# Filling the spread tile of a selective scan from SBUF instead of through DRAM, with ScalarE issuing the transfers

## The chip, the cores and the metric

The kernel runs on one core of one Trainium2 chip. The metric is the time of one execution on the device in microseconds (us); the kernel before was run three times, and the median counts. A profile of one further execution belongs to it, and all rows below come from that.

## The reference, cut to what matters

The program computes `x + s * silu(g)` for 2 sequences of 1024 tokens and 512 features in float32. `s` is a Mamba-like selective scan on the normalised input, with 1024 inner channels and 16 states per channel; `g` is a mixture of 8 experts of which each token uses 2. The part that the change touches is the scan:

```python
dt = softplus(ts @ W_dt.T + b_dt)          # one step size per token and channel
def step(state, inp):
    dt_t, B_t, C_t, u_t = inp
    dA = exp(dt_t[..., None] * A)          # 16 decays per channel
    state = state * dA + (dt_t * u_t)[..., None] * B_t[:, None, :]
    return state, einsum('bdn,bn->bd', state, C_t)
```

Every channel's `dt` and `dt * u` are needed 16 times, once for each of its 16 states.

## The kernel before, in words

**Tiling.** The 2048 tokens are cut into 4 chunks of 512 (two chunks to a sequence), and the 1024 inner channels into 8 groups of 128. One group in one chunk is called a tile; there are 32, numbered n = 8c + t for chunk c and group t. A tile needs 128 channels x 16 states x 512 tokens of recurrence. The 128 SBUF partitions hold 32 channels x 4 states at a time, so a tile takes 16 scans of 128x512: 4 quads (q = 0 to 3, the states) with 4 blocks each (r = 0 to 3, the channels, 32 at a time). A quad has a running number m = 4n + q.

**The spread tile.** The scans want each channel's row four times over, on four neighbouring partitions. `dtu` holds, on one partition per channel, two rows of 512 numbers: `dt` and `u`, which is dt times x. `rep` holds the same data spread: four blocks r, in each of them 32 channels x 4 copies on the 128 partitions. `rep` has two halves, used by even and odd tiles. It comes about in these steps for tile k:

- VectorE makes `dt` in PSUM and `u` in SBUF (`times_x`, L1163 to L1172).
- ScalarE copies `dt` from PSUM into `dtu` (`keep_dt`, L781 to L785), and stores `dtu` to the DRAM tensor `rep_rows` with one DMA of 512 KB (`keep_rows`, L861 to L866).
- SyncE (SP) waits for that store (`s_dtu`), and for tiles from 2 on also for the last reader of the half (`decay_ok`, `drive_ok`), and issues four DMAs of 512 KB from `rep_rows`, each reading 32 rows of 4 KB four times (`spread`, L415 to L423). They report to `s_rep`, two of them to each of its two semaphores.

`dtu` exists once. So both writers of the next tile's `dtu`, `times_x` on VectorE and `keep_dt` on ScalarE, wait until the store of the tile before has landed.

**The scan of a quad m.** POOL (GpSimd) multiplies the u half of `rep` by B into `drive`, 128x2048 at once (`drives`, L594 to L606, a ring of 4 slots, each free again when TensorE has summed it). ScalarE makes the decays, `exp(A * dt)`, from the dt half of `rep` into four PSUM banks `sc`, two banks at a time (`decays(m, h)`, L799 to L819): it waits for VectorE's product that last read the banks, copies the last state out, and runs two exponentials. VectorE scans (`scan(m, r)`, L1194 to L1209), and VectorE or POOL multiplies by C (L1217; `low_products` L618). TensorE sums the states into `y_ps` (`sums`, L1496 to L1502), and VectorE multiplies by the gate (`gate_tile`, L1225 to L1229).

**Everything beside it.** In the gaps of each tile TensorE also projects the next chunk's x (L1396), the gate (L1460), the expert slots (L1474, L1485) and the output (L1532). ScalarE does the convolution's first tap and x copies (`copy_x`, L715 to L729), the softplus of the tile after next (`softplus`, L777), SiLU between two loads of its function table (L956 to L970), copies of expert slots (L828, L837) with their stores (L844), and more. VectorE does three convolution taps (L1136) for each group of the next chunk.

**What sets the order.** All engines' orders are written out by hand, one stream each. SP's stream is a single one as well: a wait in it holds back all loads behind it. In a tile n the ScalarE stream is: `decays(m, 1)`, `keep_dt(n+1)`, copy of an expert slot, `diagonal(n)`, `keep_rows(n+1)`, a store of an expert slot, `decays(m+1, 0)`, `copy_x` in some tiles, `decays(m+1, 1)`, `copy_slot_T`, `decays(m+2, 0)`, table load, SiLUs, table load, `decays(m+2, 1)`, and so on (L925 to L996). In the last group of a chunk `keep_dt` and `keep_rows` come behind `decays(m+1, 0)`. SP's stream in a tile has `spread(n+1)`, then the load of the gate's weights, then expert slots and their weights (L483 to L546). At the start, before tile 0, VectorE runs `rms(0)`, `step_sizes(0)`, `route_ranks()`, `step_sizes(1)`, `route_rows()` and then the first scans (L1255 to L1265); SP issues `spread(0)` behind the stores of the normalised rows `xn_rows` (`s_xn`) and the transposes (`tr_mm`), which read the memory of `rep` under its other name `x_in` (L471 to L481).

Of the kernel before, what the change touches and what calls it, by code (L numbers as in the profile page):

```python
# [5 lines left out]
F32 = mybir.dt.float32  # L6
# [5 lines left out]
P = 128  # L12
# [3 lines left out]
TC = 512  # L16
# [100 lines left out]
def scan_moe(nc, x, wx_in, wg_in, wdt_in, wxp, wring, gate_w, means, a_log, conv_w, conv_b, d_skip,  # L117
             route_consts, bc_dram, rep_rows, xn_rows, xnT_rows, slot_x, slot_rows, s_rows, out):
    with ExitStack() as ctx:
# [6 lines left out]
        def sem(name):  # L126
            return ctx.enter_context(nc.semaphore(name))
# [127 lines left out]
        s_wdt = sem("s_wdt")  # L255
        s_dtu = sem("s_dtu")
        s_wr = [sem(f"s_wr{s}") for s in range(2)]
# [66 lines left out]
        def drives_done(eng, count):  # L324
            eng.wait_ge(drive_ok, count)
# [8 lines left out]
        def rep_landed(eng, k):  # L334
            for h in range(2):
                eng.wait_ge(s_rep[k % 2][h], REP // 2 * (k // 2 + 1))

        @block.sync
        def _(sp):
# [74 lines left out]

            def spread(k):  # L415
                sp.wait_ge(s_dtu, 16 * (k + 1))
                if k >= 2:
                    sp.wait_ge(decay_ok, UNITS * (k - 1))
                    drives_done(sp, NQ * (k - 1))
                for r in range(NR):  # L420
                    rows = rep_rows[k % 2, CH * r:CH * (r + 1), :].rearrange("c (o f) -> c o f", o=1)
                    sp.dma_start(rep[:, k % 2, r, :, :].rearrange("p k t -> p (k t)"),
                                 rows.broadcast_to([CH, NG, 2 * TC])).then_inc(s_rep[k % 2][r // 2], 16)  # L423

            def store_rows(c):
# [48 lines left out]
            sp.wait_ge(tr_mm, 16)  # L474
            spread(0)
            spread_c(0, 0)
# [6 lines left out]
            for n in range(TILES):  # L483
# [23 lines left out]
                if n + 1 < TILES:  # L507
                    spread(n + 1)
                    load_w_g(n + 1)
# [188 lines left out]
        def _(act):  # L698
# [82 lines left out]
            def keep_dt(k):  # L781
                act.wait_ge(dt_ok, k + 1)
                if k:
                    act.wait_ge(s_dtu, 16 * k)
                act.copy(dt, dt_ps[:, :]).then_inc(dt_cp, 1)  # L785
# [74 lines left out]

            def keep_rows(k):  # L861
                act.wait_ge(dt_cp, k + 1)
                act.wait_ge(dt_ok, k + 1)
                if k >= 2:
                    rep_landed(act, k - 2)
                act.dma_start(rep_rows[k % 2], dtu[:, :, :].rearrange("p k t -> p (k t)")).then_inc(s_dtu, 16)  # L866

# [48 lines left out]
            keep_dt(0)  # L916
            keep_rows(0)
            softplus(1)
# [6 lines left out]
            for n in range(TILES):  # L925
# [16 lines left out]
                if t < NT - 1:  # L942
                    keep_rows(n + 1)
                store_slot(b, left_slot)
# [4 lines left out]
                if chunk_end:  # L949
                    keep_dt(n + 1)  # L950
                    keep_rows(n + 1)
                if early is not None:
# [49 lines left out]
        def _(dve):  # L1002
# [160 lines left out]
            def times_x(k):  # L1163
                c, t = divmod(k, NT)
                if pe_log(k):
                    dve.wait_ge(log_mm, pe_logs(k + 1))
                else:
                    dve.wait_ge(sp_ok, k + 1 - pe_logs(k))
                dve.wait_ge(x_ok, k + 1)
                if k:  # L1170
                    dve.wait_ge(s_dtu, 16 * k)
                dve.tensor_tensor(u, dt_ps[:, :], xy[:, c % 2, t, :], ALU.mult).then_inc(dt_ok, 1)  # L1172
# [11 lines left out]
            def plus_log(k):  # L1184
                dve.wait_ge(part_ok, 2 * (k - pe_logs(k)) + 2)
                dve.tensor_tensor(dt_ps[:, :], t_l[:, :], dt_ps[:, :], ALU.subtract).then_inc(sp_ok, 1)

            def step_sizes(k):
                larger_part(k)
                less_rounding(k)  # L1190
                plus_log(k)
                times_x(k)

            def scan(m, r):  # L1194
                n, q = divmod(m, NQ)
                c, t = divmod(n, NT)
                if m == 0 and r == 0:
                    dve.wait_ge(first_half, 1)
                elif m == 0 or r == 0:
                    drives_done(dve, m + 1)  # L1200
                follows = c % PER_ROW > 0
                if follows:
                    dve.wait_ge(state_ok, kept_states(m - NQ * NT) + r // 2 + 1)
                lo = column(t, q, r)
                to = drive[:, m % RING, r, :] if r < 2 and on_pool(m) else sc[:, r, :]
                dve.wait_ge(decay_ok, NR * m + r + 1)
                dve.tensor_tensor_scan(to, sc[:, r, :], drive[:, m % RING, r, :],  # L1207
                                       state[:, lo:lo + 1] if follows else 0.0,
                                       ALU.mult, ALU.add).then_inc(scan_ok, 1)  # L1209
# [47 lines left out]
            route_ranks()  # L1257
            step_sizes(1)
            route_rows()
            scan(0, 0)  # L1260
            scan(0, 1)
# [434 lines left out]
```

## Time and profile before

| | |
|---|---|
| Median of three runs | 1053.31 us (1052.16, 1053.31, 1054.01) |
| The profiled execution, its own time | 1050.33 us |
| Its span, first to last instruction | 1048.4 us |
| Mean granted TensorE clock | 0.914 |
| Busy: VectorE (DVE) | 983.2 us of the span |
| Busy: POOL | 904.9 us |
| Busy: TensorE (PE) | 853.0 us |
| Busy: ScalarE (ACT) | 728.4 us |

How to read it. Busy time counts instructions that compute; waits, register work and the issue of DMAs are not in it. A queue's own work, as a DMA issue, stands in the trace under the engine's name with a q (ACTq, SPq), with the time for which it holds the engine. "Idle before, releaser" says how long the engine had nothing to run and whose end let it go on. A DMA has a time to landing, counted from its issue to its semaphore. The chain of waits goes back from the last instruction through what released each step.

### The profile page before, as it was taken

What the parts mean: (1) busy time and instruction counts of PE and PEld (TensorE: products, weight loads), DVE (VectorE), ACT (ScalarE), POOL (GpSimd) and SP (SyncE); (2) the same over time, 40 slices, a digit from 0 to 9 for tenths busy, and PEclk for the clock granted to TensorE, in tenths of its full rate; (3) what the DMA queues carried; (4) which work ended last, traced back from release to release, by engine and by line L of the source; (5) the groups of instructions that cost most, each with busy time, mean ns of one, the idle gap of its engine ahead of it and who ended that gap; (6) DMA issues with size and microseconds to landing.
All of it is one profiled execution on the core that took longest, in us unless ns stands there. A gap on an engine that the chain in (4) does not pass through costs nothing.

```text
span 1048.4 us, 10364 instructions
## 1 busy us (share of the span) xinstructions
PE 853.0 (81%) x2756; PEld 317.2 (30%) x2756; DVE 983.2 (94%) x1027; ACT 728.4 (69%) x1281; POOL 904.9 (86%) x320
## 2 busy tenths in 40 slices
PE   8945458989878998999746859989888979988478
PEld 5321113333323343333211313333323323323123
DVE  6779999999999999999999899999999997999996
ACT  3656757888877767888664566888778775767543
POOL 0616899989989998998898988899988989999996
PEclk9986669999989999999976869999999998999778
DMA  9948559887779666675843753866548575664735
GB/s 335 350 154 311 203 200 354 294 298 272 264 271 336 226 226 243 240 276 203 282 116 144 212 209 121 309 236 233 203 178 308 204 255 191 237 237 171 283 54 144
DMA packets 86585, 245.93 MB, mean 235 GB/s; under 512 B 9344, under 2 KB 10752, under 8 KB 79872
## 3 DMA queue, kind: packets, MB, share of 16 engines
q1 hardware_dynamic: 67712, 197.03, 53.0%
q10 hardware_dynamic: 12672, 31.46, 7.6%
q0 software_dynamic: 6144, 16.78, 6.0%
q8 instruction: 23, 0.38, 0.1%
q14 instruction: 34, 0.28, 0.1%
HBM read 183.11 MB, written 62.13 MB: 234 GB/s over the span
## 4 chain that ended last, share of the span: by engine, by line
POOL 22%; DVE 21%; PE 20%; issue 12%; ACT 12%; DMA 10%; SPq 2%; ACTq 0%; DVEq 0%; POOLq 0%
POOL drive L605 13%; DVE sc_ps L1207 7%; DMA rep<-rep_rows 5%; POOL drive L618 4%; ACT sc_ps L818 4%; DVE drive L1207 4%; DVE drive L1217 4%; PE x_ps L1532 3%; PE dt_ps L1460 3%; DMA rep_rows<-dtu 3%; PE f_ps L1485 3%; PE y_ps L1500 2%; PE x_ps L1396 2%; POOL slot_x L569 2%; POOL moe L590 1%
## 5 line engine op out<-in xcount | busy, mean ns | idle before, releaser
L605 POOL TENSOR_TENSOR drive<-rep,b_all 128x2048 f32<-128x2048 f32 x127 | 579.6, 4603 | 37.6 <-DMA rep<-rep_rows 34.0
L818 ACT ACTIVATE sc_ps<-rep,a_neg 128x512 f32<-128x512 f32 x512 | 332.2, 681 | 101.8 <-DVE drive L1217 72.1
L1500 PE MATMUL y_ps<-drive,stack 128*32 128x512 f32 x1024 | 151.6, 668 | 104.1 <-DVE drive L1217 66.2
L618 POOL TENSOR_TENSOR drive<-drive,c_all 128x1024 f32<-128x1024 f32 x92 | 219.8, 2389 | 11.8 <-ACT state L797 9.7
L1207 DVE TENSOR_TENSOR_SCAN sc_ps<-sc_ps,state,drive 128x512 f32<-128x512 f32 x164 | 202.5, 1272 | 5.6 <-ACT sc_ps L818 3.9
L1207 DVE TENSOR_TENSOR_SCAN sc_ps<-sc_ps,drive 128x512 f32<-128x512 f32 x164 | 193.5, 1214 | 10.2 <-ACT sc_ps L818 6.1
L1217 DVE TENSOR_TENSOR drive<-sc_ps,c_all 128x1024 f32<-128x1024 f32 x164 | 199.2, 1215 | 2.8
L1485 PE MATMUL f_ps<-w_ring,xT_slot 128*128 128x512 f32 x368 | 173.0, 614 | 23.4 <-ACT xT_slot L828 22.9
L1460 PE MATMUL dt_ps<-xnT,w_g 128*128 128x512 f32 x232 | 125.1, 689 | 24.1 <-ACT dtu L785 24.1
L1207 DVE TENSOR_TENSOR_SCAN drive<-sc_ps,state,drive 128x512 f32<-128x512 f32 x92 | 113.7, 1267 | 6.6 <-ACT sc_ps L818 6.6
L1207 DVE TENSOR_TENSOR_SCAN drive<-sc_ps,drive 128x512 f32<-128x512 f32 x92 | 109.7, 1208 | 2.0 <-POOL drive L605 0.9
L1485 PEld LDWEIGHTS f_ps<-w_ring,xT_slot 128*128 128x128 f32 x368 | 68.5, 194 | 125.0 <-issue 123.3
L1396 PE MATMUL x_ps<-xnT,w_x 128*128 128x512 f32 x192 | 88.2, 602 | 2.2 <-DMA w_x<-wx_in 1.9
L1532 PE MATMUL x_ps<-w_out,xy 128*128 128x512 f32 x176 | 83.2, 617 | 0.0
L1500 PEld LDWEIGHTS y_ps<-drive,stack 128*32 128x32 f32 x1024 | 21.5, 112 | 197.5 <-issue 140.9
L1460 PEld LDWEIGHTS dt_ps<-xnT,w_g 128*128 128x128 f32 x232 | 48.5, 220 | 105.2 <-issue 105.2
L797 ACT ACTIVATE state<-sc_ps 128x2 f32<-128x2 f32 x82 | 13.8, 169 | 65.9 <-DVE drive L1217 65.6
L1396 PEld LDWEIGHTS x_ps<-xnT,w_x 128*128 128x128 f32 x192 | 35.0, 190 | 54.7 <-issue 51.9
L1532 PEld LDWEIGHTS x_ps<-w_out,xy 128*128 128x128 f32 x176 | 33.1, 195 | 49.9 <-issue 49.3
L828 ACT COPY xT_slot<-f_ps 128x512 f32<-128x512 f32 x46 | 26.5, 576 | 28.3 <-PE f_ps L1474 28.3
L1437 PE MATMUL dt_ps<-dt_in,w_dt 128*128 128x512 f32 x64 | 39.9, 708 | 5.4 <-DVE dt_in L1252 4.2
L640 POOL TENSOR_SCALAR rep<-rep,moe 128x512 f32<-128x512 f32 x8 | 16.5, 2065 | 30.5 <-DVEq L1154 30.5
(189 smaller groups left out, 1048.8 us busy)
## 6 DMA issues: line engine op xcount, KB each, us to landing
rep<-rep_rows SPq DMA_DIRECT2D x128, 512.0 KB, 6.2
w_ring<-wring SPq DMA_DIRECT2D x46, 1024.0 KB, 6.3
rep_rows<-dtu ACTq DMA_DIRECT2D x32, 512.0 KB, 3.1
x_slot<-slot_x SPq DMA_DIRECT2D x46, 256.0 KB, 6.7
slot_rows<-y_slot ACTq DMA_DIRECT2D x46, 256.0 KB, 4.4
w_g<-wg_in SPq DMA_DIRECT2D x32, 256.0 KB, 7.1
w_x<-wx_in SPq DMA_DIRECT2D x24, 256.0 KB, 4.3
slot_x<-zeros SPq DMA_DIRECT2D x1, 5888.0 KB, 20.6
```

What stands on the lines that cost most here:

```text
L605: pool.tensor_tensor(drive[:, m % RING, :, :], rep[:, n % 2, :, 1, :], b_all[:, q:q + 1, :].broadcast_to([P, NR, TC]), ALU.mult).then_inc( ...
L618: pool.tensor_tensor(drive[:, m % RING, 0:2, :], drive[:, m % RING, 0:2, :], c_all[:, q:q + 1, :].broadcast_to([P, 2, TC]), ALU.mult).then ...
L818: act.activation(sc[:, r, :], rep[:, n % 2, r, 0, :], ACT.Exp, scale=a_neg[:, lo:lo + 1]).then_inc(decay_ok, 1)
L828: act.copy(xT_slot[:, :, :], f_ps[:, :].rearrange("p (k t) -> p k t", k=HK)).then_inc(xt_ev, 1)
L1207: dve.tensor_tensor_scan(to, sc[:, r, :], drive[:, m % RING, r, :], state[:, lo:lo + 1] if follows else 0.0, ALU.mult, ALU.add).then_inc(s ...
L1217: dve.tensor_tensor(drive[:, m % RING, 2 * h:2 * h + 2, :], sc[:, 2 * h:2 * h + 2, :], c_all[:, q:q + 1, :].broadcast_to([P, 2, TC]), ALU. ...
L1396: last = pe.matmul(x_bank(j), w(h), xnT[:, c % 2, h, :], start=(h == 0), stop=(h == HK - 1))
L1437: pe.matmul(dt_ps[:, :], w_dt[:, t, :], dt_in[:, :], start=True, stop=True).then_inc(dt_mm, 1)
L1460: mm = pe.matmul(gate_bank(c, t)[:, :], w_g[:, h, :], xnT[:, c % 2, h, :], start=(h == 0), stop=(h == HK - 1))
L1485: last = pe.matmul(f_ps[:, :], xT_slot[:, h, :], w_ring[:, j % 2, h, :], start=(h == 0), stop=(h == HK - 1))
L1500: last = pe.matmul(y_ps[CH * r:CH * (r + 1), :], stack[:, :], drive[:, m % RING, r, :], start=False, stop=(m % NQ == NQ - 1))
L1532: last = pe.matmul(bank, xy[:, c % 2, t, P * i:P * (i + 1)], w_out[:, t, :], start=(t == 0), stop=(t == NT - 1))
```

## The change

The store of `dtu` to DRAM and the tensor `rep_rows` go, and so does the semaphore `s_dtu`. The four DMAs that fill `rep` read `dtu` in SBUF, 32 partitions each, four times over. They are issued from ScalarE's stream, where the store was issued. ScalarE takes over the waits for the last reader of the half. Both writers of `dtu` now wait until the `rep` of the tile before has landed (`rep_landed`), which is when `dtu` is read out. At the start ScalarE takes over the waits for `s_xn` and `tr_mm`, and `times_x(1)`, which now has to wait for `rep` of tile 0, is moved behind `route_rows()`.

```diff
-        s_dtu = sem("s_dtu")
...
-            def spread(k):
-                sp.wait_ge(s_dtu, 16 * (k + 1))
-                if k >= 2:
-                    sp.wait_ge(decay_ok, UNITS * (k - 1))
-                    drives_done(sp, NQ * (k - 1))
-                for r in range(NR):
-                    rows = rep_rows[k % 2, CH * r:CH * (r + 1), :].rearrange("c (o f) -> c o f", o=1)
-                    sp.dma_start(rep[:, k % 2, r, :, :].rearrange("p k t -> p (k t)"),
-                                 rows.broadcast_to([CH, NG, 2 * TC])).then_inc(s_rep[k % 2][r // 2], 16)
...
             sp.wait_ge(s_xn, 16 * 16)
             sp.wait_ge(tr_mm, 16)
-            spread(0)
             spread_c(0, 0)
...
                 if n + 1 < TILES:
-                    spread(n + 1)
                     load_w_g(n + 1)
...
             def keep_dt(k):
                 act.wait_ge(dt_ok, k + 1)
                 if k:
-                    act.wait_ge(s_dtu, 16 * k)
+                    rep_landed(act, k - 1)
                 act.copy(dt, dt_ps[:, :]).then_inc(dt_cp, 1)
...
-            def keep_rows(k):
+            def spread(k):
+                act.wait_ge(dt_ok, k + 1)
                 act.wait_ge(dt_cp, k + 1)
-                act.wait_ge(dt_ok, k + 1)
                 if k >= 2:
-                    rep_landed(act, k - 2)
-                act.dma_start(rep_rows[k % 2], dtu[:, :, :].rearrange("p k t -> p (k t)")).then_inc(s_dtu, 16)
+                    act.wait_ge(decay_ok, UNITS * (k - 1))
+                    drives_done(act, NQ * (k - 1))
+                for r in range(NR):
+                    rows = dtu[CH * r:CH * (r + 1), :, :].rearrange("c k (o t) -> c o (k t)", o=1)
+                    act.dma_start(rep[:, k % 2, r, :, :].rearrange("p k t -> p (k t)"),
+                                 rows.broadcast_to([CH, NG, 2 * TC])).then_inc(s_rep[k % 2][r // 2], 16)
...
             keep_dt(0)
-            keep_rows(0)
+            act.wait_ge(s_xn, 16 * 16)
+            act.wait_ge(tr_mm, 16)
+            spread(0)
...
                 if t < NT - 1:
-                    keep_rows(n + 1)
+                    spread(n + 1)
...
                 if chunk_end:
                     keep_dt(n + 1)
-                    keep_rows(n + 1)
+                    spread(n + 1)
...
             def times_x(k):
...
                 if k:
-                    dve.wait_ge(s_dtu, 16 * k)
+                    rep_landed(dve, k - 1)
...
             route_ranks()
-            step_sizes(1)
+            larger_part(1)
+            less_rounding(1)
+            plus_log(1)
             route_rows()
+            times_x(1)
```

## Rows read from the trace of the kernel before

**Rows 1.** The page, busy time of each engine.
```profile
PE 853.0 (81%) x2756; PEld 317.2 (30%) x2756; DVE 983.2 (94%) x1027; ACT 728.4 (69%) x1281; POOL 904.9 (86%) x320
```

**Rows 2.** VectorE's waits: line, releaser, us in total, times, longest.
```profile
DVE sc_ps L1207 <- ACT sc_ps L818: 10.1, 11, 2.0
...
DVE drive L1207 <- ACT sc_ps L818: 7.3, 8, 4.0
...
DVE sc_ps L1207 <- POOL drive L605: 4.6, 4, 2.1
```

**Rows 3.** POOL's waits, the same columns.
```profile
POOL drive L605 <- DMA rep<-rep_rows: 34.0, 13, 8.3
```

**Rows 4.** The four fills (L422) and the store (L866): issue ns min/median/max, landing.
```profile
L422 SPq DMA_DIRECT2D rep<-rep_rows x128: 513/598/932, 68.2 to 982.7; - x128
...
L866 ACTq DMA_DIRECT2D rep_rows<-dtu x32: 326/326/348, 65.4 to 976.9; - x32
...
DMA to landing us min/median/max: 2.6/3.1/8.8
```

**Rows 5.** Timeline, DMA issues on SP; L367 copies SBUF rows four times over.
```profile
267.22 2.46 SPq L422 DMA_DIRECT2D rep<-rep_rows  x4
...
270.37 0.43 SPq L367 DMA_DIRECT2D slot_x<-zeros  x1
...
295.49 1.82 SPq L431 DMA_DIRECT2D b_all<-bc_rows  x3
```

**Rows 6.** Timeline, VectorE where it waited: start, us, instruction, idle before.
```profile
249.08 2.35 DVE L1207 TENSOR_TENSOR_SCAN sc_ps<-sc_ps,drive 128x512 f32<-128x512 f32 x2 [0.75 <-ACT sc_ps L818]
...
599.38 3.46 DVE L1207 TENSOR_TENSOR_SCAN sc_ps<-sc_ps,drive 128x512 f32<-128x512 f32 x3 [2.12 <-POOL drive L605]
...
878.88 2.46 DVE L1207 TENSOR_TENSOR_SCAN drive<-sc_ps,state,drive 128x512 f32<-128x512 f32 x2 [4.04 <-ACT sc_ps L818]
```

**Rows 7.** Timeline: POOL's first drive of a tile, two of 13 stalls; one store ahead.
```profile
540.79 0.33 ACTq L866 DMA_DIRECT2D rep_rows<-dtu  x1
...
554.67 4.53 POOL L605 TENSOR_TENSOR drive<-rep,b_all 128x2048 f32<-128x2048 f32 x1 [3.23 <-DMA rep<-rep_rows]
...
852.45 4.55 POOL L605 TENSOR_TENSOR drive<-rep,b_all 128x2048 f32<-128x2048 f32 x1 [2.94 <-DMA rep<-rep_rows]
```

**Rows 8.** The chain of waits, 834 to 879 us.
```profile
834.63 7.06 DMA rep_rows<-dtu
...
843.81 8.49 DMA rep<-rep_rows
...
866.16 1.94 PE y_ps L1500 x8
```

**Rows 9.** Busy us (x count) by engine, from store to second table load; 15 stretches.
```profile
205.70:219.00 13.30, 11.68 (x35) 4.86 (x36) 13.30 (x15) 11.60 (x22) 12.09 (x4) 1.00 0.85 296
...
664.70:677.10 12.40, 11.86 (x41) 4.52 (x39) 12.37 (x14) 11.55 (x22) 9.92 (x4) 1.00 0.93 336
...
949.40:960.90 11.50, 11.50 (x42) 4.21 (x40) 9.91 (x10) 8.35 (x13) 11.50 (x5) 1.00 0.78 271
sum 175.40, PE 159.26 PEld 62.06 DVE 172.85 ACT 149.13 POOL 162.44; mean PE 10.62 PEld 4.14 DVE 11.52 ACT 9.94 POOL 10.83
```

The columns are length, then PE, PEld, DVE, ACT, POOL, TensorE's granted clock, DMA share and GB/s.

**Rows 10.** Timeline, tile 6: two waits of ScalarE, its decays, VectorE's scans of them.
```profile
269.01 0.17 ACT L797 ACTIVATE state<-sc_ps 128x2 f32<-128x2 f32 x1 [0.46 <-DVE drive L1217]
...
271.91 0.21 ACT L797 ACTIVATE state<-drive 128x2 f32<-128x2 f32 x1 [0.88 <-DVE drive L1207]
...
277.91 1.30 ACT L818 ACTIVATE sc_ps<-rep,a_neg 128x512 f32<-128x512 f32 x2
...
278.71 2.32 DVE L1207 TENSOR_TENSOR_SCAN sc_ps<-sc_ps,drive 128x512 f32<-128x512 f32 x2
```

**Rows 11.** Page, DMA issues: KB each, median us to landing.
```profile
slot_x<-zeros SPq DMA_DIRECT2D x1, 5888.0 KB, 20.6
```

More of the change, by code:

```diff
@@ L117, in scan_moe @@
 def scan_moe(nc, x, wx_in, wg_in, wdt_in, wxp, wring, gate_w, means, a_log, conv_w, conv_b, d_skip,
-             route_consts, bc_dram, rep_rows, xn_rows, xnT_rows, slot_x, slot_rows, s_rows, out):
+             route_consts, bc_dram, xn_rows, xnT_rows, slot_x, slot_rows, s_rows, out):
     with ExitStack() as ctx:
@@ L1685 @@
     bc = nc.dram_tensor("bc_rows", (NCH, 2 * N, TC), F32, kind="Internal").ap()
-    rep_rows = nc.dram_tensor("rep_rows", (2, P, 2 * TC), F32, kind="Internal").ap()
     xn_rows = nc.dram_tensor("xn_rows", (TOK, H), F32, kind="Internal").ap()
@@ L1692 @@
     out = nc.dram_tensor("out", (TOK, H), F32, kind="ExternalOutput").ap()
-    scan_moe(nc, *aps, bc, rep_rows, xn_rows, xnT_rows, slot_x, slot_rows, s_rows, out)
+    scan_moe(nc, *aps, bc, xn_rows, xnT_rows, slot_x, slot_rows, s_rows, out)
     r = run_bass_kernel_spmd(nc, [arrays], core_ids=[0])
```

## The prediction

> **What bounds the kernel now.** I read the page first: VectorE is busy 983.2 us, 94% of the span, POOL 86%, ScalarE 69% [rows 1]. So a change helps only where it takes away a wait of VectorE, and costs only where it gives VectorE a new one. VectorE's waits came next. Behind the start, most of what it waits for is ScalarE's decays, 10.1 + 7.3 us in 19 waits; POOL's drives cost it 4.6 us in 4 [rows 2]. POOL in turn stands for 34.0 us in 13 waits for the fill of `rep` [rows 3]. This is seven times what VectorE waits for POOL: with four slots in the ring most of POOL's stalls never reach VectorE. Last I read the timeline around `keep_rows`, because that is where ScalarE gets more to do.
>
> **What goes: the way through DRAM.** The store lands in 2.6 to 8.8 us [rows 4], and the fill follows it. In tile 25 the store went out at 834.63 and took 7.06 us; the last of the four fills was issued at 843.81 and landed 8.49 us later, 17.7 us in all, and POOL went on at 852.45 after a wait of 2.94 [rows 7, 8]. POOL had thus been ready 14.9 us behind the store's issue. In tile 15 the same reckoning gives 554.67 - 3.23 - 540.79 = 10.7 us, the tightest sort [rows 7]. Afterwards the path is the issue of four DMAs on ScalarE and one landing. If a fill from SBUF goes as fast as one from DRAM, that is 1.9 us to the fourth issue and about 8.5 to its landing, 10.4 us: no stall in tile 25, next to none in tile 15.
>
> How fast a fill from SBUF is, the trace does not show; no DMA in it reads a few partitions several times into SBUF. Its bounds: at the fast end the rate of the one long read of all partitions, 5888 KB in 20.6 us, 286 GB/s, so 7.3 us for four fills [rows 11]; at the slow end a quarter of that rate, since each fill reads a quarter of the partitions, 29 us. I take 10 to 12 us, near the fills that were measured, because the receiving side and the bytes are theirs.
>
> That the slow end deserves thought is what the Trainium skill says ("SBUF — State Buffer", section on the DMA port swizzle): 32 partitions reach only 8 of 16 ports, and it gives 189 GB/s for partitions 0 to 31; by its figure the four fills would take an estimated 11 us before any contention. No row here shows it.
>
> **What VectorE gets from that.** All of its 4.6 us behind POOL can go [rows 2]. The 0.75 us at 249.08 lie behind a stall of tile 5 [rows 6]. The 4.04 us at 878.88 lie on the chain that runs from the late fill through POOL, `y_ps` and the gate to ScalarE; of them the 2.94 of the stall can go [rows 6 to 8]. At the start the first fill is issued some 3 us earlier, since the store's 2.6 us go; that removes about 1 us. The sum is 4.6 + 0.75 + 2.94 + 1 = 9.3 us. I take 7, because in the tightest tiles a fill of 10 to 12 us leaves part of the stall: in tile 15 a fill 1 us late takes back 1 of the 2.12 us at 599.38 [rows 6]. The bounds are 3 and 10.
>
> **What comes: four long issues for a short one on ScalarE.** A plain issue holds its engine 0.33 us; the four fills hold SP 2.46 us, the first 0.51, those behind it 0.60 each; a single row of L431, which also spreads 32 rows to 128 partitions, says the same, 1.82 for three [rows 4, 5]. An issue that copies one row of SBUF four times on its own partition takes 0.43 behind another [rows 5]. The new form spreads 32 to 128, so I take 2.46. ScalarE gets 2.46 - 0.33 = 2.13 us more a tile, 68 us over 32 fills, of which its waits have to swallow what VectorE is not to see.
>
> Tile 6 shows how. Behind the issue ScalarE waits 0.46 and 0.88 us for VectorE, which swallow 1.34. Then come the first table load, the SiLUs and the second table load, and then the decays at 277.91. Their first exponential ends at about 278.6 and VectorE's scan starts at 278.71 [rows 10]: no slack. So 2.13 - 1.34 - 0.1 = 0.7 us reach VectorE. I followed each tile like this, from its `keep_rows` on, taking off every wait of ScalarE and the slack before each scan, and taking what VectorE was given as given, so that it isn't counted twice. 17 tiles swallow everything. 15 do not: tiles 4 to 8, 12, 13, 15, 19 to 24 and 29. Over their stretches ScalarE is busy 149.1 of 175.4 us; of the 26.3 left, the DMA issues, one or two in each and 0.33 long, take some 8, so that about 18 us of waits stand against 15 x 2.13 = 32 us, and 14 remain; the slacks take another 3 [rows 9]. Result: 11 us. The worst is tile 19, 11.55 busy of 12.40, nothing left but issues: 1.9 us arrive [rows 9]. The cost is steep in the issue's price: with 1.5 us more a tile the same reading gives 4 us, with 1.0 it gives 1, with 2.5 it gives 17. Bounds 1 and 17.
>
> **The rest, at nothing.** SP loses four issues and a wait a tile and so sends weights earlier; nobody waits noticeably for these loads, and the price without cover is a later fill by shared bandwidth, which is in its range. `spread`'s waits on ScalarE are for decays it made itself and drives that VectorE has already begun to scan; behind them stand the slot's store and `decays(m+1, 0)`, which would wait too. `keep_dt` and `times_x` wait for a fill that the running tile has already read. At the start, `times_x(1)` goes behind `route_rows`, the same work in another order, and softplus(1) starts 1.2 us later under the routing work. SP no longer waits for the first store and sends its 4 MB of staging up to 3 us earlier, beside the first fill; that can cost the 1 us counted as gain.
>
> **The sum.** -7 + 11 = +4 us on the profiled execution, 1050.33 to 1054.3. That execution lies 3 us below the median of 1053.31, so the forecast is 1057.3.
>
> **Rivals.** *ScalarE has the room, and the kernel gets faster.* If an issue from SBUF costs 0.43, as that of L367 [rows 5], the four take 1.7 and add 1.3 a tile. The cost is then 2 to 3 us against 8 of gain: 1053.3 - 5.5 = 1048. It decides at about 1.8 us more a tile, where cost and gain are both 7. For it speaks that L367 is the only broadcast from SBUF; against it, that its rows stay on their partition.
> *The fill is slow.* If 32 partitions feed it at half rate, four fills take 7.3 x 2 = 14.6 us [rows 11] and the landing is 16 us behind the first issue. POOL is ready after 10.7 in the tight tiles: stalls of 5 us in about ten, where they are 1 to 4 now. Gain 2, and 4 to 8 us more reach VectorE: +4 + 5 + 6 = +15, 1068. At the quarter rate every tile would stall 10 us or more, over 1200; I leave that outside. The rule of the Trainium skill named above points this way, though by its figure the fill would still land at about 13 us.
> *Nothing measurable.* Gain and cost come out equal, near 8 us each, both within their bounds: 1053.
>
> **How the numbers follow.** Forecast, ScalarE's issues outweigh the shorter path: 0.43, own range 1055.4 to 1062. Faster: 0.28. No change: 0.16, that is within 0.2% or 2.1 us, about what a measurement of this kernel can tell from none. Slow fill: 0.13. Slower by over 0.2% is 0.43 + 0.13 = 0.56. The range reaches from 1046, the faster rival with the full 10 us of gain against 3, to 1067, just short of the slow fill.
>
> **What the profile after would show.** Right: no `rep_rows`; L866's place holds four issues of 2.4 to 2.5 us together; ScalarE's waits for VectorE's L1217 shrink by tens of us; VectorE's waits for L818 rise from 17 to some 25 us, the new ones behind the second table load; POOL's 34.0 us fall below 10. Wrong: issues under 0.45 each (the faster rival), POOL waiting 40 us or more for `rep` with landings above 12 us (the slow fill), or a VectorE that waits more for POOL than for ScalarE.

## The result, and the profile after

The changed kernel takes 1309.65 us (median of 4, 1304.28 to 1315.69) against 1052.91 us (median of 4): the ratio is 1.2439, 95% interval 1.2381 to 1.2497. That is 257 us slower. The forecast was 1057.3 in a range of 1046 to 1067. The sign was right and the size wrong by far.

The page of the kernel after, busy time of each engine, answers to [rows 1]:

```profile
span 1306.1 us, 10334 instructions
...
PE 899.7 (69%) x2756; PEld 337.2 (26%) x2756; DVE 988.9 (76%) x1027; ACT 725.8 (56%) x1281; POOL 905.2 (69%) x320
```

VectorE and ScalarE do the same work, VectorE in 988.9 us against 983.2, so all but some 6 of the 257 us are waits. TensorE does the same work too, in 899.7 us against 853.0, at a mean granted clock of 0.831 against 0.914; the run below that only holds ScalarE (e6) has 0.837. These are the waits of the kernel after (engine, line, releaser: us in total, times, longest); L805 is the decays' line, L856 the fills', L831 the slot stores':

```profile
PE f_ps L1481 <- ACT xT_slot L815: 215.6, 25, 14.5
DVE drive L1200 <- ACT sc_ps L805: 171.2, 31, 11.0
...
ACT sc_ps L805 <- issue: 154.9, 16, 12.2
ACT state L784 <- issue: 150.8, 16, 13.7
...
POOL drive L605 <- ACT state L784: 93.5, 14, 12.4
...
DVE sc_ps L1200 <- ACT sc_ps L805: 65.2, 23, 7.4
...
POOL drive L592 <- DMA rep<-dtu: 22.9, 5, 7.0
```

VectorE waits 236 us for ScalarE's decays, against 17.4 [rows 2]. ScalarE stands still for "issue", 306 us in 32 waits, about one to a tile: it waits for no semaphore, it is issuing a DMA. TensorE and POOL wait for ScalarE as well. POOL's waits for `rep`, on which half of the forecast turned, have even fallen, from 34.0 [rows 3] to 22.9 us: at this pace the fills are rarely late.

The issues themselves, on the line of the fills and then on the line of the slot stores (ns min/median/max; below it the us to landing), answer to [rows 4]:

```profile
L856 ACTq DMA_DIRECT2D rep<-dtu x128: 550/868/4395, 65.6 to 1226.4; - x128
...
DMA to landing us min/median/max: 6.2/10.2/18.7
```

```profile
L831 ACTq DMA_DIRECT2D slot_rows<-y_slot x46: 326/362/5767, 177.5 to 1230.2; - x46
```

The median hides it; one tile shows it. ScalarE's timeline of the kernel after, tile 6 (start, us, instruction, idle before):

```profile
309.54 0.57 ACTq L856 DMA_DIRECT2D rep<-dtu  x1
...
310.14 7.89 ACTq L856 DMA_DIRECT2D rep<-dtu  x3
318.08 5.77 ACTq L831 DMA_DIRECT2D slot_rows<-y_slot  x1
323.89 0.21 ACT L784 ACTIVATE state<-drive 128x2 f32<-128x2 f32 x1 [13.64 <-issue]
```

And VectorE's of the same stretch:

```profile
312.71 1.21 DVE L1210 TENSOR_TENSOR drive<-sc_ps,c_all 128x1024 f32<-128x1024 f32 x1
324.92 1.23 DVE L1200 TENSOR_TENSOR_SCAN drive<-sc_ps,drive 128x512 f32<-128x512 f32 x1 [11.00 <-ACT sc_ps L805]
```

The first two issues of this tile take 0.57 and 0.62 us, as forecast. The third takes 3.9 and the fourth 3.3, and a store of an expert slot that has nothing to do with `rep` takes 5.8 us, because it is next on the same queue (with the fills on SyncE, in e1 below, it takes 0.33 again). As long as an issue lasts, the engine that issues does nothing else: the three slow ones are most of the 13.64 us. Summed over the trace the fills' issues take 246.6 us and the slot stores' 86.9; the store of `dtu` and the slot stores took 10.4 and 15.3 before. That is 9.6 us more a tile.

A second loss stands at the start. `times_x(1)` now waits until the fill of tile 0 has landed:

```profile
85.30 0.69 DVE L1165 TENSOR_TENSOR dtu<-dt_ps,xy 128x512 f32<-128x512 f32 x1 [6.88 <-DMA rep<-dtu]
```

The first scan of tile 0 begins at 85.9 us and not at 77.9, 8.0 us of the 257.

### The profile page after: what moved, and what is told of

It is laid out like the page before. It is cut to its first block and busy times, and to the rows that moved or that the text cites. A ratio compares the mean times of both kernels' runs of the same rounds, so it can differ in the third digit from the quotient of the medians.

```text
span 1306.1 us, 10334 instructions
## 1 busy us (share of the span) xinstructions
PE 899.7 (69%) x2756; PEld 337.2 (26%) x2756; DVE 988.9 (76%) x1027; ACT 725.8 (56%) x1281; POOL 905.2 (69%) x320
## 5 line engine op out<-in xcount | busy, mean ns | idle before, releaser
L805 ACT ACTIVATE sc_ps<-rep,a_neg 128x512 f32<-128x512 f32 x512 | 331.2, 681 | 234.5 <-issue 154.9
L1481 PE MATMUL f_ps<-w_ring,xT_slot 128*128 128x512 f32 x368 | 219.7, 753 | 215.6 <-ACT xT_slot L815 215.6
L1481 PEld LDWEIGHTS f_ps<-w_ring,xT_slot 128*128 128x128 f32 x368 | 86.9, 247 | 344.4 <-issue 344.3
L1456 PE MATMUL dt_ps<-xnT,w_g 128*128 128x512 f32 x232 | 121.3, 672 | 32.4 <-ACT dtu L772 32.4
L1496 PEld LDWEIGHTS y_ps<-drive,stack 128*32 128x32 f32 x1024 | 21.6, 112 | 205.2 <-issue 170.6
L784 ACT ACTIVATE state<-drive 128x2 f32<-128x2 f32 x46 | 9.2, 200 | 105.1 <-issue 100.0
L1129 DVE SCALAR_TENSOR_TENSOR x_ps<-x_pad,cw,x_ps 128x512 f32<-128x512 f32 x54 | 40.2, 744 | 17.0 <-ACT x_ps L714 16.5
## 6 DMA issues: line engine op xcount, KB each, us to landing
rep<-dtu ACTq DMA_DIRECT2D x128, 512.0 KB, 10.2
slot_x<-zeros SPq DMA_DIRECT2D x1, 5888.0 KB, 20.6
```

Of the source, the lines that this page charges most:

```text
L805: act.activation(sc[:, r, :], rep[:, n % 2, r, 0, :], ACT.Exp, scale=a_neg[:, lo:lo + 1]).then_inc(decay_ok, 1)
L1129: dve.scalar_tensor_tensor(out=x_bank(j) if k < K - 1 else xy[:, c % 2, t, :], in0=padded(j)[:, k:k + TC], scalar=cw[:, t * K + k:t * K + ...
L1456: mm = pe.matmul(gate_bank(c, t)[:, :], w_g[:, h, :], xnT[:, c % 2, h, :], start=(h == 0), stop=(h == HK - 1))
L1481: last = pe.matmul(f_ps[:, :], xT_slot[:, h, :], w_ring[:, j % 2, h, :], start=(h == 0), stop=(h == HK - 1))
L1496: last = pe.matmul(y_ps[CH * r:CH * (r + 1), :], stack[:, :], drive[:, m % RING, r, :], start=False, stop=(m % NQ == NQ - 1))
```

## The experiments

Each experiment has a short name, e1 to e10 for kernels and m1, m2 for transfers alone. All times are medians in us; "before" is the kernel before, run beside each on the same chip. Its single runs there lie between 1047.6 and 1056.0, which says how much a difference of a few us between single runs is worth.

### Who holds ScalarE: the source or the queue

e2: only the source of the fills changed, ScalarE issues them:

```diff
+            act.dma_start(first_rep, dtu[:, :, :].rearrange("p k t -> p (k t)")).then_inc(s_dtu, 16)
+            act.wait_ge(s_dtu, 16)
             spread(0)
...
-                    rows = dtu[CH * r:CH * (r + 1), :, :].rearrange("c k (o t) -> c o (k t)", o=1)
+                    rows = first_rep[CH * r:CH * (r + 1), :].rearrange("c (o f) -> c o f", o=1)
```

> The changed kernel with the source of the fills alone exchanged: ScalarE issues the same four DMAs in the same places, but they read 128 rows of 4 KB of a DRAM tensor that is written once, with dt and u of tile 0; so every tile gets the dt and u of tile 0. Theory A (the source is slow): four issues take 2.4 to 2.6 us together, landings 6 to 7 us, and the time is 1050 to 1070 us. Rival B (ScalarE's queue holds fewer transfers than SyncE's, or fills on it are slow in themselves): four issues still take 7 to 9 us and the time stays above 1250 us.

Measured: 1085.0 (one run) against 1049.9. The issues and landings of its fills:

```profile
L857 ACTq DMA_DIRECT2D rep<-first_rep x128: 520/625/1420, 73.7 to 1011.1; - x128
...
DMA to landing us min/median/max: 3.4/6.4/13.9
```

The four issues take 2.4 us in nearly every tile, the very price of the forecast. So ScalarE issues these fills as fast as SyncE did, and the source makes the hold. The time is higher than expected. About 12 us of the 35 are this experiment's own late start: ScalarE waits for the one store, and the first scan begins at 90.3 us instead of 77.9. The other 23 us I put down to the 2.1 us more on ScalarE a tile, less what the shorter path gives back; e10 below, which holds ScalarE 2.4 us, loses 21.6.

e1: the other way round, SyncE issues (`spread` moves to its stream, with its waits) and the source is SBUF:

```diff
             def spread(k):
-                act.wait_ge(dt_ok, k + 1)
+                sp.wait_ge(dt_ok, k + 1)
...
                 if n + 1 < TILES:
+                    spread(n + 1)
                     load_w_g(n + 1)
```

> The changed kernel with its four fills issued by SyncE instead of ScalarE; they still read dtu in SBUF. Theory A (a fill from 32 partitions of SBUF drains slowly, about 4 us each, and the third and fourth issue hold whichever engine issues them until an earlier fill has drained): SyncE's issues of a tile take 7 to 9 us together, as ScalarE's did (7.9 in tile 5 of the changed kernel), the landings stay near 10 us, but ScalarE is free, its slot stores take 0.33 us again, and the kernel comes back to 1060 to 1110 us, with POOL waiting 50 to 150 us for rep. Rival B (it is ScalarE's queue that is slow, not the source): SyncE's issues take 2.5 us together, landings 6 to 7 us, and the time is at or below that of the kernel before, 1040 to 1053 us.

Measured: 1107.12 against 1049.91, ratio 1.0538 (1.0494 to 1.0582). Issues, landings and POOL's waits:

```profile
L422 SPq DMA_DIRECT2D rep<-dtu x128: 547/902/4665, 65.7 to 1039.9; - x128
...
DMA to landing us min/median/max: 6.7/9.9/20.1
```

```profile
POOL drive L605 <- DMA rep<-dtu: 90.1, 17, 12.3
```

The hold follows the source to SyncE: the four issues in tile 1 take 0.55, 0.60, 4.07 and 2.01 us, and in 26 of 32 tiles the third takes 3.9 us or more. There it holds back loads and not decays, and 200 of the 257 us are gone. The other 57 I put down to a second fault: the fills land late, and POOL, no longer slowed by ScalarE, now waits 90 us for them. VectorE's waits bear most of that out: it waits 32.4 us for POOL's drives instead of 5.5, and 14.0 instead of 5.5 for TensorE's sums behind them; another 11.5 us are for a part of the softplus that TensorE adds, in four tiles. The loads held back on SyncE cost little: TensorE's waits for DMAs (matmuls and weight loads) are 16.9 us against 11.7. From the first issue of a tile to the last landing the trace has a median of 9.3 us before, 17.2 in the changed kernel, 16.5 here, and 10.0 with the source in DRAM.

### Does the hold by itself make the 257 us

e6: the kernel before, with ScalarE held by copies that nobody needs.

```diff
+            def hold():
+                for _ in range(29):
+                    link(act.activation(held[:, :], ident[:, :], ACT.Copy))
...
                     keep_rows(n + 1)
+                    hold()
```

> The kernel before, with ScalarE held by 29 copies of 128x128 in a row behind keep_rows in each tile (31 times), about 9.8 us each; nothing else is changed. In the changed kernel ScalarE spends 246.6 us on the fills' issues and 86.9 us on the slot stores behind them, against 10.4 and 15 us before: 9.6 us more a tile. Theory A (the hold of ScalarE by itself makes the loss): 1270 to 1330 us, VectorE waiting 200 us or more for ScalarE's decays. Rival E (the loss needs the slow landings of the data too): under 1200 us.

Measured: 1293.1 (one run) against 1052.1, with `rep` filled from DRAM as ever. VectorE's waits in it:

```profile
DVE drive L1214 <- ACT sc_ps L819: 147.0, 27, 8.6
...
DVE sc_ps L1214 <- ACT sc_ps L819: 73.2, 19, 7.9
```

Holding ScalarE for 9.9 us a tile, 306 us in all against 308 more in the changed kernel, costs 241 us, 94% of the loss, and makes the same waits, 220 us against 236. Theory A holds: the hold alone makes this much. The 8.0 us of the late start are not in it.

### Two queues with two fills each

e4:

```diff
-                for r in range(NR):     # on ScalarE
+                for r in (0, 1):        # on ScalarE
...
+                for r in (2, 3):        # on SyncE
```

> The changed kernel with blocks 0 and 1 (partitions 0 to 63) still issued by ScalarE and blocks 2 and 3 (64 to 127) by SyncE, both reading dtu in SBUF. If the hold is of a queue with two slow transfers in it, neither queue ever has a third: ScalarE's two issues take 1.2 us together and SyncE's as well, as the first two of a tile do now. If blocks 0 and 1 and blocks 2 and 3 read through different ports, both pairs drain at once, all four land within 9 us of the first issue, and the time is 1055 to 1085 us; if all reads of SBUF share one narrow place, the four still take 15 us, POOL waits as much for rep as with SyncE alone (90 us), and the time is 1095 to 1130 us.

Measured: 1163.3 (one run) against 1052.1, outside both ranges. The reason is in the slot stores' line:

```profile
L844 ACTq DMA_DIRECT2D slot_rows<-y_slot x46: 326/334/5709, 165.7 to 1083.2; - x46
```

The slot store behind ScalarE's two fills was the third transfer there and was held up to 5.7 us, 84.8 us in all. The fills were held too: only in 15 of 32 tiles did ScalarE's two go out in 1.2 to 1.6 us, and in 15 others the second took 2.2 to 3.1 us, with one fill ahead of it on its own queue; in 13 of these SyncE's two were in flight, while in six of the seven tiles in which SyncE had none in flight it took 0.62 us. So the other queue's transfers count too. The four fills took 15.7 us to the last landing, against 17.2 and 16.5 on one queue: a second queue adds hardly any speed.

### Which rows are read

Every fourth partition, ScalarE issues (e3); neighbours in another order, SyncE issues (e8); and every second partition, SyncE issues (e9):

```diff
-                    rows = dtu[CH * r:CH * (r + 1), :, :]...
+                    rows = dtu[r::NR, :, :]...              # e3
+                    rows = dtu[at:at + 63:2, :, :]...       # e9, at = r % 2 + 64 * (r // 2)
-                for r in range(NR):
+                for r in (0, 2, 1, 3):                      # e8
```

> The changed kernel with one change: fill r reads the partitions r, r + 4, r + 8 and so on of dtu, not the 32 neighbours from 32 r on. Bytes, rows and copies are the same, the reads are spread over all 128 partitions; the channels reach the wrong places. Theory C (32 neighbouring partitions are behind few ports, the narrow place is there): fills go about twice as fast, four issues take 3 to 5 us together, the median landing falls from 10.2 to 6 to 7 us, and the time falls to 1060 to 1150 us. Rival D (reading SBUF row by row four times over is slow wherever the rows lie, or two transfers of a queue that read SBUF cannot overlap): issues stay at 7 to 9 us and the time above 1250 us.

e3 measured: 1109.5 (one run) against 1049.9, and for the fills:

```profile
L856 ACTq DMA_DIRECT2D rep<-dtu x128: 531/680/2037, 65.5 to 1035.7; - x128
...
DMA to landing us min/median/max: 3.0/5.1/11.8
```

Same bytes, same number of rows and copies, and the landing falls from 10.2 to 5.1 us, below the 6.2 of a fill from DRAM; four fills take 8.5 us instead of 17.2. The issues fall from 7.7 or so to 3.4 us a tile. With the slot stores behind them ScalarE is still held 3.7 us more a tile than before, and the kernel is 60 us slower; between e10 below (2.4 us, 21.6) and e6 (9.9 us, 241) a straight line gives an estimate of some 60.

> The kernel of e1 (SyncE issues the four fills from 32 neighbouring partitions each) with the order of the blocks 0, 2, 1, 3 instead of 0, 1, 2, 3. If neighbouring blocks 0 and 1 share their ports and 2 and 3 the other ones, two transfers in flight now use different ports: the third issue no longer takes 4 us, the four issues fall from 7.3 to 3 to 5 us and the time from 1107 to 1060 to 1090 us. If a transfer is limited by itself, by whatever it reads from, or the engines go through one transfer after the other, nothing changes: 1095 to 1120 us.

e8 measured: 1081.2 (one run) against e1's 1107.1. The time lies in the first case's range, but not for its reason: the issues did not fall (250.9 us in all, 232.9 in e1). The four fills took 15.2 us instead of 16.5, and POOL waited 55.4 instead of 90.1 us. Landings 1.3 us sooner in e1's 17 stalls are an estimated 22 of these 35 us; the rest is not explained.

> The kernel of e1 (SyncE issues, source in SBUF) with every second partition as source: block 0 reads 0, 2, to 62, block 1 the odd ones, blocks 2 and 3 the same from 64 on; the channels reach the wrong places. Theory C (number of ports): no change against e1, fills take 15 to 17 us and the time is 1095 to 1115 us. Rival G (adjacent DMA engines that read through one port): fills near 9 us, 1040 to 1055 us.

e9 measured: 1064.0 (one run) against 1050.8; four fills took 13.8 us. It lies between the theories: faster than neighbours, and far from every fourth.

### The fills alone

m1:

> Only transfers, no scan and no result: fills of 512 KB one at a time (32 rows of 4 KB, each four times) from neighbouring partitions 0 to 31, from every second of 0 to 62, from every fourth of 0 to 124, and from DRAM; a plain copy of 128 partitions to 128; two halves of a fill from every fourth partition, straight and with the source halves swapped; then four in a row of each sort. In the kernels the four fills took 17.2 us from the first issue to the last landing from neighbours, 9.3 from DRAM, 8.5 from every fourth. Theory C (the number of ports that the 32 source rows reach): one fill takes about 5.5 us from neighbours and as long from every second row (both reach half of the ports), 3.5 us from every fourth; swapped halves are as fast as straight ones; blocks 0 and 2 in turn are faster than 0, 1, 2, 3. Rival F (a DMA engine reads slowly when its source lies elsewhere than its destination; rows of every fourth partition happen to lie where they are written): swapped halves take as long as neighbours. Rival G (two DMA engines reading through one port stand in each other's way): every second row is faster than neighbours. The third of four issues from neighbours is held by 3 us or more here too, with nothing else in flight; from DRAM it is not.

Each sort four times, one transfer at a time (kernel line: issue ns, then us to landing): L40 neighbours, L44 every second, L48 every fourth, L52 DRAM.

```profile
L40 SPq DMA_DIRECT2D dst<-src x4: 542/543/684, 2.0 to 20.4; - x4
DMA to landing us min/median/max: 6.0/6.1/6.3
...
L44 SPq DMA_DIRECT2D dst<-src x4: 520/528/559, 26.5 to 39.2; - x4
DMA to landing us min/median/max: 4.2/4.2/4.2
...
L48 SPq DMA_DIRECT2D dst<-src x4: 523/532/547, 43.4 to 52.6; - x4
DMA to landing us min/median/max: 3.0/3.0/3.1
...
L52 SPq DMA_DIRECT2D dst<-x x4: 535/544/594, 55.7 to 67.1; - x4
DMA to landing us min/median/max: 3.6/3.8/3.9
```

Then four in a row, from the timeline: L70 neighbours, L74 every fourth, L78 DRAM, L82 neighbours in the order 0, 2, 1, 3, L103 and L87 two on each of two queues, L92 plain copies from 128 partitions to 128 (start, length of the issues):

```profile
116.01 7.73 SPq L70 DMA_DIRECT2D dst<-src  x4
130.18 3.49 SPq L74 DMA_DIRECT2D dst<-src  x4
137.31 2.50 SPq L78 DMA_DIRECT2D dst<-x  x4
145.71 7.97 SPq L82 DMA_DIRECT2D dst<-src  x4
159.00 2.97 ACTq L103 DMA_DIRECT2D dst<-src  x2
159.05 1.19 SPq L87 DMA_DIRECT2D dst<-src  x2
173.09 3.23 SPq L92 DMA_DIRECT2D dst<-src  x4
```

Each group starts when the one before has landed, so the differences of the starts are the times: 14.2 us for four from neighbours, 7.1 from every fourth partition, 8.4 from DRAM, 13.3 in the other order, 14.1 on two queues, 6.8 for the plain copies. With nothing else in flight the issues take 7.7 us as in the kernel. It is the fill, not contention. On two queues three of the four issues go out in 0.5 to 0.6 us, and ScalarE's second, the last of the four, takes 2.3: as in e4, the other queue's transfers count. The two halves with the source halves exchanged landed in 3.5 us against 3.6 straight: rival F falls.

m2:

> Only transfers again. In m1 one fill of 32 rows took 6.1 us from neighbouring partitions, 4.2 from every second, 3.0 from every fourth: above 2 us that is 4.1, 2.2 and 1.0, in proportion to the source rows in each aligned group of four partitions (4, 2, 1). Theory H (such a group hands out one row at a time): 16 rows of 256 KB take 2 + 4 us from 0 to 15, 2 + 2 from every second of 0 to 30, 2 + 1 from every fourth of 0 to 60 and also from every eighth; 32 rows from 64 to 95 take 6.1, from 2 to 33 as long, from every third 3.5 to 4. Theory C (ports as the Trainium skill numbers them): of the 16-row fills those from every second, fourth and eighth partition reach 8 ports with 2 rows each and take the same time. If the proportion was chance, 256 KB from every second of 0 to 30 take under 3.4 us. Eight issues in a row: from DRAM all at 0.5 to 0.7 us; from neighbours the third and each later one 3 to 4 us, on ScalarE (six in a row) as on SyncE.

Landings, one at a time: 16 rows from 0 to 15 took 4.3 us, from every second 3.0, every fourth and every eighth 2.9; 32 rows from 64 on 6.1, from 2 on 5.9, every third 4.6, every fourth 3.0. Theory H is wrong in its sizes (6, 4 and 3 us were expected for the first three). Theory C fits these 16-row fills, every second, fourth and eighth partition alike, but not the 32-row ones of m1, where it expected neighbours and every second row to take the same: 6.1 and 4.2 us. Four in a row from every second partition took 11.9 us. Eight in a row, L76 from DRAM and L80 from neighbours, and six on ScalarE, L93:

```profile
145.48 5.45 SPq L76 DMA_DIRECT2D dst<-x  x8
159.37 18.49 SPq L80 DMA_DIRECT2D dst<-src  x8
185.27 13.22 ACTq L93 DMA_DIRECT2D dst<-src  x6
```

One by one the eight issues from neighbours take 0.56, 0.60, 3.93, 2.88, 2.70, 2.42, 2.53 and 2.57 us, those on ScalarE 0.60, 0.63, 3.97, 2.89, 2.60 and 2.38, and from DRAM none takes over 0.78. So in a row on one queue the first two go out, and from the fourth on each issue takes 2.4 to 2.9 us, about as long as the landings lie apart (2.8), on either engine. That a transfer drains more slowly than it is issued is not enough for a hold: the eight from DRAM land 1.2 to 1.8 us apart, and the last goes out in 0.66 us with seven ahead of it, six of them not yet landed. In m1 and m2 all transfers that were held read SBUF, plain ones too: of the eight stores of 512 KB from SBUF to DRAM that end m1 and m2, the fourth and each later one take 1.2 us to issue, and they land 1.2 to 1.4 us apart. What in the chip keeps an issue out is not shown.

### What ScalarE's time costs

> The kernel before, with ScalarE held by five copies of 128x128 in a row, each waiting for the one before, behind keep_rows in each tile (31 times), some 2.2 us in all; nothing else is changed. My prediction's reading of the timeline says that 2.1 us more a tile cost 11 us, 2.5 us cost 17: 1062 to 1070 us against 1053. Rival: the waits behind the hold swallow more than I took off, and it costs under 4 us; or they feed back through TensorE and POOL, and it costs over 25 us.

e5 measured: 1060.67 against 1049.91, ratio 1.0094 (1.0064 to 1.0124), so 10.8 us. The hold was 1.7 us, not 2.2, since the copies follow each other faster than I had thought; my reading gives 6 us for that.

> The kernel before with ScalarE held by 7 copies instead of the 5 of e5, about 2.4 us a tile. My prediction's reading gave 17 us for 2.5 us and 4 us for 1.5; e5 measured 10.8 us for a hold that the trace shows as 1.7 us, about twice the reading. If the reading is low by that factor, this costs 24 to 32 us (1074 to 1084); if e5's surplus was a fixed sum of 5 us, it costs 19 to 23 us; e2, whose issues hold ScalarE 2.1 us longer, lost 22 us outside its late start.

e10 measured: 1072.38 against 1050.77, ratio 1.0207 (1.0182 to 1.0231), so 21.6 us. My reading gives 15 to 16. It is low by 5 to 7 us in both, and the waits of this kernel show what it left out:

```profile
DVE sc_ps L1214 <- ACT sc_ps L819: 13.3, 13, 2.0
DVE drive L1214 <- ACT sc_ps L819: 12.9, 16, 3.0
DVE x_ps L1143 <- ACT x_ps L728: 11.4, 14, 1.4
```

The last row is the convolution's first tap, which ScalarE makes in `copy_x` behind the hold. Before, VectorE waited for it once, 1.1 us at 40 us, ahead of the first scan, and nowhere behind. I had followed the decays alone. In e5 the waits for them rise by 6.1 us, as the reading says, and those for the taps by 4.8; here it is 8.8 and 10.3, so part of what I gave to the decays is taken by the taps.

### A version that beats both

This is e7. e3 says that the rows should lie four apart, e1 that SyncE should issue. Both together, with results that are the reference's: the channels of x, `dt` and `u` are put on the partitions so that block r's 32 channels sit on every fourth partition. The scans and sums see them where they always were, and the skip's diagonal matrix puts x back in order.

```diff
-                    rows = dtu[CH * r:CH * (r + 1), :, :]...   # issued by SyncE, as in e1
+                    rows = dtu[r::NR, :, :]...
...
-                act.activation(diag[:, :], ident[:, :], ACT.Copy,
+                act.activation(diag[:, :].rearrange("p (r c) -> p r c", r=NR),
+                               ident[:, :].rearrange("p (c r) -> p r c", r=NR), ACT.Copy,
...
+    mix = np.arange(P).reshape(NR, CH).T.reshape(P)    # applied to wx_in, w_dt, w_x, conv_w, conv_b, d_skip
```

> Fills from SBUF issued by SyncE, each from every fourth partition, with the channels of x, dt and u put on the partitions so that the results are the reference's (weights permuted on the host, the permutation undone by the skip's diagonal matrix); nothing is added on the device. Theory: the reads spread over all ports land in 5.5 us (e3), there is no store ahead of them, ScalarE has one issue less a tile than in the kernel before, and SyncE has its 2.5 to 3.5 us of issues. So the stalls of POOL for rep, 34 us before, fall below 10, VectorE gets back the 7 to 9 us of my prediction's first part, and the time is 1038 to 1048 us against 1050. Rival: SyncE's longer issues hold its loads of weights and slots, or the fills run into w_ring's loads: 1050 to 1065 us.

Measured: 1042.79 (1041.75 to 1043.42, 6 runs) against 1052.06, ratio 0.9909 (0.9891 to 0.9927): 9.3 us faster. Its waits and its fills:

```profile
POOL drive L605 <- DMA rep<-dtu: 16.0, 6, 9.2
...
DVE sc_ps L1197 <- ACT sc_ps L818: 9.6, 11, 2.0
DVE drive L1197 <- ACT sc_ps L818: 4.5, 5, 2.5
...
DVE sc_ps L1197 <- POOL drive L605: 3.3, 2, 1.8
```

```profile
L422 SPq DMA_DIRECT2D rep<-dtu x128: 530/650/3077, 65.5 to 973.0; - x128
...
DMA to landing us min/median/max: 3.0/5.4/15.7
```

POOL's wait for `rep` halves, from 34.0 [rows 3] to 16.0 us, of which 9.2 are one fill at the start beside the staging; behind that fill it falls from 25.7 to 6.8. VectorE's waits for ScalarE's decays and POOL's drives fall from 22.0 [rows 2] to 17.4, of which 3.3 are the decays and 1.3 the drives, and those for TensorE's sums from 5.5 to 3.4. Tile 25, whose late fill led to the 4.04 us at 878.88 [rows 6, 8], has no stall of POOL now, and VectorE waits 2.46 us there. The two profiles differ by 7.4 us; the rest of the 9.3 is the difference between profiled executions and medians.

## Why the prediction was wrong, and where it was right

**What bounds the kernel: right.** VectorE is busy 982.7 to 988.9 us in every kernel here; what changed are its waits, and whoever held ScalarE held VectorE.

**What goes, 7 us of gain within 3 to 10: right in size, but not in this kernel, and in part by luck.** It takes a fill as fast as one from DRAM. With such a fill (e7) the gain is 9.3 us in the medians and 7.4 between the profiles, although part of it may come from the store that ScalarE no longer issues. Scan by scan e7 gains some 1.0 us at the start, 0.9 around 249.08 and 2.8 around 878.88, as the terms said (1, 0.75, 2.94). But of the 4.6 us behind POOL that I let go whole only 1.3 went: the 2.12 us at 599.38 are still 1.79. So that the gain equals my sum before the deduction is chance. (The 5888 KB in 20.6 us are 293 GB/s and not 286, which changes nothing.)

**"I take 2.46": the step that failed.** I priced the issues by what they take on SyncE from DRAM [rows 4, 5]. That is exact for DRAM on ScalarE (e2: 2.4 us), and wrong from SBUF: 7.7 us, and 2.2 more for the slot stores behind, 9.6 more a tile instead of 2.13. The cause is that I took an issue for a fixed price. Behind two or three transfers that read SBUF it has none, as m1 and m2 show. e6 shows that this hold by itself makes 241 of the 257 us. I had named as the one uncertainty whether it is 0.43 or 0.60 us; the bounds had no case in which the source of a transfer, rather than its form, sets how long the issuing engine stands. I let a slow fill cost something on POOL alone, and nothing on the engine that issues it.

**"I take 10 to 12 us" for the fill: mis-sized.** Four fills took 17.2 us in the kernel and 14.2 alone, against 9.3 from DRAM before. My argument, that the receiving side and the bytes are the same, was the wrong side to look at. By the half rate that I had ruled a rival it would have been 14.6. The kernel of e1, which has this fill without the hold of ScalarE, is 57 us slower and not 15; POOL stalled in 17 tiles and not in ten.

The Trainium skill's rule on ports ("SBUF — State Buffer", section on the DMA port swizzle) pointed the right way, and its 189 GB/s for partitions 0 to 31 fit: in a row of eight, the fills of 512 KB from the third to the seventh landed 2.8 us apart, 187 GB/s. But the count of ports does not explain the fills of 32 rows taken alone: every second partition of 0 to 62 reaches the same 8 ports by its map and took 4.2 us against 6.1, and every third, which reaches more, took 4.6. Here the measurement decides, and the rule is not the whole cause.

**"Result: 11 us" for 2.13 us more on ScalarE: low.** Measured were 10.8 us for 1.7 and 21.6 for 2.4. The reading was right in that the cost climbs steeply, and left out the taps of the convolution. With it right, the forecast from [rows 4, 5] would have been some 5 to 8 us higher, of no weight beside 257.

**The rest at nothing: right for SyncE's loads, wrong for the start.** I had priced the move of `times_x(1)` as the same work in another order. But it then waits for the whole first fill, 6.9 us, and the first scan begins 8.0 us late; in e1, where the fill is as slow and SyncE issues it, the wait is 3.1 us and the scan 2.8 us late, and in e7 neither is there.

**Left open:** what in the reading of SBUF makes neighbouring partitions slow (ports, adjacent DMA engines, groups of four: each explains some of the patterns and none all), what stops the third issue, why fills from DRAM are not held, and a part of what the order 0, 2, 1, 3 gives POOL. I did not try an issue from POOL.

## What to carry to other kernels

An engine that issues a DMA can do nothing else while the issue lasts, and behind transfers that read SBUF this can be long: here two fills in a row were free and the third cost 4 us, and what came behind it on that queue paid as well. So a row of such transfers must not be issued by the engine that the critical one waits for. Eight fills from DRAM in a row did not have it. Look in the profile for waits on "issue" and for the maximum of an issue's time, not its median. When a DMA reads 32 SBUF partitions four times over, as here, choose them four apart: with SyncE issuing, it cost a permutation of the weights and turned a loss of 57 us into a gain of 9.

## What was not expected of the hardware

A fill from 32 neighbouring partitions of SBUF is slower than the same fill from DRAM, 6.1 against 3.8 us alone, and one from every fourth partition faster than both, 3.0. The issue of the third such fill takes 3.9 us on SyncE and 4.0 on ScalarE with nothing else in flight, while eight fills from DRAM in a row go out at 0.6 to 0.8 us each. Spreading the fills over two queues changes nothing, 14.1 against 14.2 us, and the second on ScalarE's queue is still held 2.3 us. Stores of 512 KB from SBUF to DRAM are held too, from the fourth on, 1.2 us each.
